# Moving the second group's later statistics chain, and the token weights, in a convolution and scan kernel on one core

## The chip, the cores and the metric

The kernel runs on one core of a Trainium2 chip. The metric is device time in microseconds (us) from the start to the end of one execution. TensorE (PE), VectorE (DVE), ScalarE (ACT), GpSimd (POOL) and the SyncE queue (SP) each run their own list of instructions in order, and wait for one another by semaphores.

## The reference

Input x is 16 images of 256 channels by 1024 pixels, all float32. Two residual blocks follow one another, each behind a group norm (32 groups of 8 channels):

```python
x = x + L0(gn(x))          # mean over pixels -> softmax gate over 8 experts -> sigmoid scale per channel
x = x + L1(gn(x))
# L1, for each image:
xz = silu(in_proj_w @ x + in_proj_b)              # 256 -> 3 * 256: x_ssm, res, gate
xf = silu(depthwise_conv3(x_ssm) + dw_b)
dbc = dbc_w @ xf + dbc_b                          # dt, B, C for 2 heads, 8 states each
xf, dt, B, C = the same in a scan order of the pixels, per head, got by sorting a Moebius map
h[n] = exp(dt[n] * A) * h[n-1] + dt[n] * B[n] * xf[n];  y[n] = C[n] . h[n] + D * xf[n]
y = y back in pixel order
out = silu(out_proj_w @ (y * silu(gate) + res) + out_proj_b)
```

L0 only multiplies each channel of an image by a number. So both group norms and L0 come down to a few parameters for each image and channel, which need the mean and the mean square of every channel of the image first.

## The kernel before, in words

The images are worked on in eight phases of two (`NB = 2`, `PH = 8`), one *cycle* each. In the setup each image is loaded once for its statistics alone. VectorE takes them with `bn_stats` (four passes of 512 elements for two tiles of channels), and for the first `BY_ACT = 5` phases the second tile is taken by ScalarE instead, with two passes of 1024 elements (`statistics(i, b)`, L533 and L534). SP's queue loads the images; phases 6 and 7 go into buffers that phases 3 and 4 used and wait for `stats_done` and `stats_done_a`.

From the statistics come the parameters, in two groups: group 0 is the first four images, group 1 the other twelve. For each group there is a chain of tiny steps across three engines: `combine` (VectorE), `group_sums` (TensorE, a matmul that averages over the channels of a norm group), `normed`, `routes`, `routed`, `experts` and so on for L0; and then the *later chain* for the second norm: `rescaled` (VectorE), `group_sums(g, V_STATS2)` (TensorE), `group_variance` (VectorE), `deviation` (ScalarE, a square root with a table load of its own), `scaled` (VectorE), `shifts` (TensorE, 12 small products), `biases` (VectorE), and `take_params(2)`, which hands phase 2 its parameters, on which GpSimd's `scale_x(2)` waits. For group 1 the matmuls write the PSUM bank `pj[3]`.

The scan over 1024 pixels is done in chunks of 16. For each cycle i and head h:

- `segments(i, h)` on TensorE and `decays(i, h)` on ScalarE make the exponentials (8 activations of 400 elements into `big`). `decays` waits until the scans of the last head are done (`hs_ready`), whose decay factors it overwrites.
- `factors(i, h)` on VectorE makes `bblk`, `turned_factors` makes `cblk`.
- `chunk_sums(i, h, b)` on TensorE (L1411, 8 matmuls with `bblk`) writes the bank `st`, and `scans(i, h, b)` on VectorE runs 8 scans from it into `hs`. There is one bank `st`, so the next `chunk_sums` waits for the last scans.
- `token_products`, `token_weights` and `weights_block` on VectorE build `mblk`, the weights of pixels inside a chunk.
- `results(i, h)` on TensorE: `within` (L1432, with `mblk`), `turn` (L1422, L1423) which transposes `cblk` and `hs` and whose copies ScalarE makes in `turned` (L653), and `from_states` (L1442), which waits for those copies. ScalarE copies the result to `rs` (`result`), and SP stores it.

The order on each engine is written out by hand in its `cycle(i)`. TensorE also has the projections (`project`, `gate`, `residual`, all L1366), `rows` (L1386 and L1388, whose results ScalarE copies in `rows_out`) and `output` (L1491). GpSimd scatters those rows to scan order (`scatter`) and gathers the results back.

## Time and profile before

| what | value |
|---|---|
| median of 3 runs | 877.38 us (875.68 to 877.74) |
| the profiled execution | 875.38 us, of which the profile's span is 872.9 us |
| TensorE busy | 794.8 us (91%) |
| VectorE busy | 571.8 us (66%) |
| ScalarE busy | 557.0 us (64%) |
| GpSimd busy | 372.9 us (43%) |
| mean granted clock of TensorE | 0.96 of full |

The span begins with the first instruction and ends with the last; the execution's own time includes what lies around it. Busy times overlap between engines, so they do not add up to the span. A high busy share is an average over setup, cycles and end, and says nothing of which wait ends last in one of them.

### The profile page before, as it was taken

What the parts mean: (1) busy time and instruction counts of PE and PEld (TensorE: products, weight loads), DVE (VectorE), ACT (ScalarE), POOL (GpSimd) and SP (SyncE); (2) the same over time, 40 slices, a digit from 0 to 9 for tenths busy, and PEclk for the clock granted to TensorE, in tenths of its full rate; (3) what the DMA queues carried; (4) which work ended last, traced back from release to release, by engine and by line L of the source; (5) the groups of instructions that cost most, each with busy time, mean ns of one, the idle gap of its engine ahead of it and who ended that gap; (6) DMA issues with size and microseconds to landing.
All of it is one profiled execution on the core that took longest, in us unless ns stands there. A gap on an engine that the chain in (4) does not pass through costs nothing.

```text
span 872.9 us, 11238 instructions
## 1 busy us (share of the span) xinstructions
PE 794.8 (91%) x3854; PEld 513.4 (59%) x3854; DVE 571.8 (66%) x1048; ACT 557.0 (64%) x1056; POOL 372.9 (43%) x325
## 2 busy tenths in 40 slices
PE   2689867999999999999999999999999999988996
PEld 1356557745675566645684576645684576654852
DVE  5798398467783769276774769275964759178724
ACT  6776645587647856587647846677648846654552
POOL 2394306760288107840388108840487008610240
PEclk9689858999999999999999999999999999999999
DMA  8824671567738293658638393749539463775242
GB/s 330 334 97 149 170 100 62 156 199 84 232 133 238 51 184 141 187 168 98 219 132 241 59 220 114 192 140 134 191 124 256 59 139 125 203 150 134 71 123 97
DMA packets 110986, 136.06 MB, mean 156 GB/s; under 512 B 41801, under 2 KB 91602, under 8 KB 110930
## 3 DMA queue, kind: packets, MB, share of 16 engines
q1 hardware_dynamic: 97040, 99.11, 44.8%
q0 software_dynamic: 12288, 35.80, 12.3%
q8 instruction: 31, 0.51, 0.3%
q10 hardware_dynamic: 1602, 0.45, 0.3%
q14 instruction: 25, 0.20, 0.1%
HBM read 82.76 MB, written 53.61 MB: 156 GB/s over the span
## 4 chain that ended last, share of the span: by engine, by line
PE 68%; ACT 11%; DVE 10%; issue 4%; POOL 4%; DMA 1%; SPq 0%; DVEq 0%; POOLq 0%
PE pj L1366 30%; PE pj L1491 9%; PE pj L1432 6%; PE st L1411 5%; PE tp L1386 5%; ACT big L630 4%; PE tp L1388 4%; PE pj L1442 3%; POOL xt_scratch L434 2%; ACT xf L610 2%; PE tp L1481 2%; DVE big L1121 2%; POOL crow L448 2%; PE tp L1422 2%; ACT L630 1%
## 5 line engine op out<-in xcount | busy, mean ns | idle before, releaser
L1366 PE MATMUL pj<-xb,inw 128*128 128x512 f32 x768 | 340.9, 598 | 0.0
L434 POOL DMA_INDIRECT xt_scratch<-stage,idx x128 | 175.6, 1372 | 344.3 <-issue 333.3
L1366 PEld LDWEIGHTS pj<-xb,inw 128*128 128x128 f32 x768 | 143.7, 191 | 167.0 <-issue 159.6
L448 POOL DMA_INDIRECT crow<-yt_scratch,idx x128 | 135.4, 1058 | 98.9 <-DMA yt_scratch<-rs 59.1
L1017 DVE SCALAR_TENSOR_TENSOR xf<-xs,small,xf 128x1024 f32<-128x1024 f32 x64 | 84.0, 1322 | 108.3 <-ACT xf L603 107.1
L1491 PE MATMUL pj<-gt,outw 128*128 128x512 f32 x256 | 118.2, 593 | 0.6 <-DVE gt L1171 0.6
L653 ACT COPY ch<-tp 128x256 f32<-128x256 f32 x128 | 42.7, 381 | 74.7 <-PE tp L1423 74.6
L1432 PE MATMUL pj<-xp,mblk 128*128 128x128 f32 x512 | 71.7, 285 | 17.0 <-ACT gt L685 8.8
L1177 DVE SCALAR_TENSOR_TENSOR xb<-xb,pcur,rs 128x1024 f32<-128x1024 f32 x32 | 41.0, 1284 | 60.3 <-ACT rs L716 60.3
L642 ACT COPY stage<-tp 128x256 f32<-128x256 f32 x128 | 47.8, 374 | 48.7 <-PE tp L1388 46.4
L1432 PEld LDWEIGHTS pj<-xp,mblk 128*128 128x128 f32 x512 | 64.7, 198 | 23.1 <-ACT gt L685 13.8
L716 ACT ACTIVATE rs<-pj,small 128x512 f32<-128x512 f32 x64 | 44.1, 695 | 49.9 <-PE pj L1491 49.8
L1386 PE MATMUL tp<-dw,xf 128*128 128x162 f32 x256 | 64.9, 338 | 12.1 <-ACT stage L643 11.2
L1386 PEld LDWEIGHTS tp<-dw,xf 128*128 128x128 f32 x256 | 47.5, 210 | 42.1 <-issue 30.9
L630 ACT ACTIVATE big<-sg,small 128x400 f32<-128x400 f32 x128 | 63.7, 609 | 10.5 <-PE sg L1397 10.3
L1491 PEld LDWEIGHTS pj<-gt,outw 128*128 128x128 f32 x256 | 45.9, 190 | 38.1 <-issue 37.0
L1411 PEld LDWEIGHTS st<-bblk,xp 128*128 128x128 f32 x512 | 61.8, 196 | 10.6 <-DVE hs L1077 7.0
L1411 PE MATMUL st<-bblk,xp 128*128 128x64 f32 x512 | 63.1, 278 | 4.0 <-DVE bblk L1103 2.8
L685 ACT ACTIVATE gt<-pj,pcur 128x512 f32<-128x512 f32 x64 | 41.8, 687 | 32.0 <-PE pj L1366 31.8
L1388 PE MATMUL tp<-dw,xf 128*128 128x162 f32 x256 | 61.0, 323 | 0.0
L1121 DVE TENSOR_TENSOR big<-big,crow 128x1024 f32<-128x1024 f32 x32 | 59.8, 1913 | 0.0
L1164 DVE TENSOR_TENSOR gt<-tp,gt 128x512 f32<-128x512 f32 x64 | 41.2, 684 | 24.5 <-PE tp L1481 23.7
(241 smaller groups left out, 1151.6 us busy)
## 6 DMA issues: line engine op xcount, KB each, us to landing
xb<-in_x SPq DMA_DIRECT2D x16, 1024.0 KB, 7.1
xp<-xt_scratch SPq DMA_DIRECT2D x8, 2048.0 KB, 12.6
crow<-cd_scratch SPq DMA_DIRECT2D x128, 128.0 KB, 8.3
yt_scratch<-rs SPq DMA_DIRECT2D x16, 1024.0 KB, 4.9
out<-xb SPq DMA_DIRECT2D x16, 1024.0 KB, 5.6
gt<-in_x SPq DMA_DIRECT2D x4, 1024.0 KB, 11.7
big<-in_x SPq DMA_DIRECT2D x4, 1024.0 KB, 12.1
xp<-xt_scratch SPq DMA_DIRECT2D x8, 272.0 KB, 8.7
```

Of the source, the lines that this page charges most:

```text
L434: pool.indirect_dma_start(out=xt_d.ap(), out_offset=bass.IndirectOffsetOnAxis(ap=idx[:, k:k + 1], axis=0), in_=v(stage, (nt * H + h) * ROW ...
L448: pool.indirect_dma_start(out=v(crow, k * NB * P, (1, NB * P)), out_offset=None, in_=yt_d.ap()[0:(h + 1) * N], in_offset=bass.IndirectOffs ...
L630: last = nc.scalar.activation(v(big, s * EEW, (1, EEW)), v(sg, 0, (1, EEW)), ACT.Exp, scale=v(small, ANEG + h * S + s, (1, 1)))
L642: nc.scalar.copy(v(stage, o + b * P, (ROW, H), (1, P)), v(tp[nt % 2], 0, (P + HK, H), (1, P)))
L1017: nc.vector.scalar_tensor_tensor(dst, tap(k), wt(k), dst, ALU.mult, ALU.add).then_inc(conv_step[ot], 1)
L1121: nc.vector.tensor_tensor(v(big, W_OFF + b * NT * L, (Q * L, S), (L, NT), (1, L)), v(big, SEG + b * NT * L, (EEW, S), (L, NT), (1, L)), v( ...
L1366: last = nc.tensor.matmul(o[:, :], v(inw, ct * 3 * C + col + ot * P, (1, P)), x_view(par, b, ct, nt * HALF, HALF), start=(ct == 0), stop=( ...
L1386: nc.tensor.matmul(v(o, 0, (1, P + HK)), tile(0), v(dw, HK, (1, P + HK)), start=True, stop=False, skip_group_check=True)
L1388: nc.tensor.matmul(v(o, P, (1, HK + P)), tile(1), v(dw, 0, (1, HK + P)), start=False, stop=True, skip_group_check=True).then_inc(x_full, 1)
L1411: last = nc.tensor.matmul(v(st, g * CPT * S, (1, CPT * S)), x_rows(h, b, g), v(bblk, (b * NT + g) * CPT * S, (1, CPT * S)), start=True, st ...
L1432: nc.tensor.matmul(v(pj[2 * b + e], gp * P, (1, P)), v(mblk, (b * NT + g) * P, (1, P)), x_rows(h, b, g), start=(gp == 0), stop=False, skip ...
L1491: last = nc.tensor.matmul(o[:, :], v(outw, h * C + ot * P, (1, P)), v(gt, (b * CT + h) * N + nt * HALF, (1, HALF)), start=(h == 0), stop=( ...
```

## The change

It has three parts, and some moves of buffers that they need.

1. The later chain of group 1 moves back. VectorE ran `rescaled(1)` and `group_variance(1)` ahead of cycle 0 and `scaled(1)` and `biases(1)` around the first head; now `rescaled(1)` and `group_variance(1)` stand behind `factors(0, 1)`, `scaled(1)` behind the scans of head 1, `biases(1)` and `take_params(2)` behind its `weights_block`. On TensorE `group_sums(1, V_STATS2)` moves from behind the first `chunk_sums` to behind `results(0, 0)`, and `shifts(1)` from ahead of `results(0, 0)` to behind the last `chunk_sums`. ScalarE's `deviation(1, V_VAR2)` moves from ahead of cycle 0 to behind the second `result` of head 0. The matmuls now write the bank `sg`, and so wait for `ee_ready`.
2. In cycle 0 and in cycle 7 VectorE makes `token_products` ahead of the first scans and the whole `mblk` ahead of the second scans of head 0.
3. `BY_ACT` is 4: ScalarE's statistics of phase 4 go to VectorE, as four more `bn_stats`, and ScalarE's statistics of image (3, 1) move behind its first `project` steps. On VectorE `statistics(4)` is split in two and moves behind `ranks`, between the bias additions.

The statistics' columns of `rs` move up behind column 2048 and the averaging matrix from `m16` to `rs` (a change of addresses; `result` now waits for `params_ready` at head 1 instead of head 0). The core of the diff:

```diff
@@ build
-        BY_ACT = 5
+        BY_ACT = 4
@@ SP: loads of phases 6 and 7
                 sp.wait_ge(stats_done, i - 2)
-                sp.wait_ge(stats_done_a, (i - 2) * NB)
+                sp.wait_ge(stats_done_a, min(i - 2, BY_ACT) * NB)
                 load_for_statistics(i)
@@ ScalarE, setup
-            for b in range(NB):
-                statistics(3, b)
+            statistics(3, 0)
...
             for ot in range(CT):
                 project(0, 0, 0, ot)
                 first_tap(0, 0, ot)
-            statistics(4, 0)
+            statistics(3, 1)
             convolved(0, 0)
             for ot in range(CT):
                 project(0, 0, 1, ot)
                 first_tap(0, 1, ot)
-            statistics(4, 1)
             rows_out(0, 0)
...
             convolved(1, 1)
-            deviation(1, V_VAR2)
@@ ScalarE, cycle
                 result(i, 0, 0)
                 turned(i, 0, range(4 + AHEAD, 8))
                 result(i, 0, 1)
+                if first(i):
+                    deviation(1, V_VAR2)
                 gate(i, par, range(4, 6))
@@ VectorE, cycle
-                scans(i, 0, 0)
-                if first(i):
-                    scaled(1)
+                if first(i) or last_phase(i):
+
+                    token_products(i, 0)
+                    scans(i, 0, 0)
+                    token_weights(i, 0)
+                    weights_block(i, 0)
+                    scans(i, 0, 1)
                 else:
+                    scans(i, 0, 0)
                     token_products(i, 0)
-                scans(i, 0, 1)
+                    scans(i, 0, 1)
                 if more:
                     add_bias(i + 1, 0, 0, NT)
                     add_bias(i + 1, 1, 0, BIAS_TILES)
                     add_bias(i + 1, 1, BIAS_TILES, BIAS_TILES)
-                token_weights(i, 0)
-                weights_block(i, 0)
+                if not first(i) and not last_phase(i):
+                    token_weights(i, 0)
+                    weights_block(i, 0)
+                factors(i, 1)
                 if first(i):
-                    biases(1, 0, 3 * CT, P_BIAS2, params_ready)
-                    take_params(i + 2)
-                factors(i, 1)
+                    rescaled(1)
+                    group_variance(1, P_SUMS2, V_VAR2)
                 token_products(i, 1)
                 token_weights(i, 1)
                 turned_factors(i, 1)
                 scans(i, 1, 0)
+                if first(i):
+                    scaled(1)
                 weights_block(i, 1)
+                if first(i):
+                    biases(1, 0, 3 * CT, P_BIAS2, params_ready)
+                    take_params(i + 2)
                 scans(i, 1, 1)
@@ VectorE, setup
             convolve(0, 1)
-            statistics(4)
             ties(1)
             ranks()
             add_bias(0, 0, 0, NT)
+            statistics(4, (0,))
+            add_bias(0, 1, 0, BIAS_TILES)
+            statistics(4, (1,))
+            add_bias(0, 1, BIAS_TILES, BIAS_TILES)
             statistics(5)
-            for lo in range(0, NT, BIAS_TILES):
-                add_bias(0, 1, lo, BIAS_TILES)
             statistics(6)
...
             begin(0)
-            rescaled(1)
-            token_products(0, 0)
-            group_variance(1, P_SUMS2, V_VAR2)
@@ TensorE, cycle
                 chunk_sums(i, 0, 0)
-                if not i:
-                    group_sums(1, V_STATS2)
                 segments(i, 1)
...
                 if i:
                     gate(i, par, range(0, 4), last)
-                else:
-                    shifts(1, range(0, CT))
-                    shifts(1, range(CT, 3 * CT))
                 last = four(g_drained, i * G_U + 4)
                 if not i:
 
-                    last[3] = (params_ready, 1)
+                    last[3] = (chain_a, A_CHAIN + A_SIGMOID)
                 results(i, 0, before_t, last, AHEAD, lambda: chunk_sums(i, 1, 0))
                 last = four(r_drained, i * R_U + 4)
+                if not i:
+
+                    pe.wait_ge(ee_ready, H)
+                    group_sums(1, V_STATS2)
                 gate(i, par, range(4, 6), last)
                 last[:2] = four(g_drained, i * G_U + 8)[:2]
                 chunk_sums(i, 1, 1)
+                if not i:
+                    shifts(1, range(0, CT))
+                    shifts(1, range(CT, 3 * CT))
                 results(i, 1, (t_drained, i * T_U + 8), last, 0, lambda: None)
```

Three places of the instruction order follow. In the changed kernel the lines of VectorE count one more, and those of TensorE ten more (L1077 is L1078 there, L1411 is L1421).

VectorE, cycle 0, head 1, from the end of `factors(0, 1)` (`bblk`) to `scans(0, 1, 0)` (`hs`), before:

```order
L1096 TENSOR_TENSOR bc<-xp,big 128x64 x2
L1103 TENSOR_TENSOR bblk<-bc,cst 128x1024
L1121 TENSOR_TENSOR big<-big,crow 128x8x128 x2
L1133 TENSOR_TENSOR big<-big,bc 128x2048
L1138 TENSOR_TENSOR big<-big 128x1024
L1138 TENSOR_TENSOR big<-big 128x512
L1142 SCALAR_TENSOR_TENSOR m<-cst,small,big 128x256
L1146 TENSOR_TENSOR m<-m,big 128x256
L1112 TENSOR_TENSOR cblk<-bc,cst 128x1024
L1077 SCALAR_TENSOR_TENSOR hs<-big,st 128x64 x8
```

The same engine and place in the changed kernel, from the last two steps of `rescaled(1)`:

```order
L966 TENSOR_TENSOR rs<-rs 128x2x12
L967 TENSOR_TENSOR rs<-rs 128x2x12
L916 COPY rs<-sg 128x2x12
L917 TENSOR_TENSOR rs<-rs 128x2x12
L918 TENSOR_TENSOR rs<-sg,rs 128x2x12
L919 TENSOR_SCALAR rs<-rs 128x2x12
L1122 TENSOR_TENSOR big<-big,crow 128x8x128 x2
L1134 TENSOR_TENSOR big<-big,bc 128x2048
L1139 TENSOR_TENSOR big<-big 128x1024
L1139 TENSOR_TENSOR big<-big 128x512
L1143 SCALAR_TENSOR_TENSOR m<-cst,small,big 128x256
L1147 TENSOR_TENSOR m<-m,big 128x256
```

Between `bblk` and `token_products` (`big<-big,crow`) now stand the eleven steps of `rescaled(1)`, of which two are shown, and the four of `group_variance(1)`, the first of which (`rs<-sg`) reads what TensorE's `group_sums` writes.

TensorE, cycle 0, from the last `from_states` of head 0 (`pj<-ch`) through two gates (`pj<-xb,inw`) to `results(0, 1)`, before:

```order
L1442 MATMUL pj<-ch 128x128 x8
L1366 MATMUL pj<-xb,inw 128x512 x4
L1411 MATMUL st<-bblk,xp 128x64 x8
L1422 MATMUL tp<-dw,cblk 128x128
L1423 MATMUL tp<-dw,hs 128x128
```

The same place in the changed kernel:

```order
L1452 MATMUL pj<-ch 128x128 x8
L1299 MATMUL sg<-rs 128x48
L1376 MATMUL pj<-xb,inw 128x512 x4
L1421 MATMUL st<-bblk,xp 128x64 x8
L1331 MATMUL sg<-rs,inw 128x12 x12
L1432 MATMUL tp<-dw,cblk 128x128
L1433 MATMUL tp<-dw,hs 128x128
```

`group_sums` (`sg<-rs`, one matmul) now stands ahead of the gates, and the twelve of `shifts` (`sg<-rs,inw`) between the last `chunk_sums` (`st<-bblk,xp`) and `results(0, 1)`.

VectorE, the start of cycle 7, behind `output(6, b)`, before:

```order
L1077 SCALAR_TENSOR_TENSOR hs<-big,st 128x64 x8
L1121 TENSOR_TENSOR big<-big,crow 128x8x128 x2
L1077 SCALAR_TENSOR_TENSOR hs<-big,st 128x64 x8
L1133 TENSOR_TENSOR big<-big,bc 128x2048
L1138 TENSOR_TENSOR big<-big 128x1024
L1138 TENSOR_TENSOR big<-big 128x512
L1142 SCALAR_TENSOR_TENSOR m<-cst,small,big 128x256
L1146 TENSOR_TENSOR m<-m,big 128x256
L1154 TENSOR_TENSOR mblk<-m,cst 128x2048
```

In the changed kernel:

```order
L1122 TENSOR_TENSOR big<-big,crow 128x8x128 x2
L1078 SCALAR_TENSOR_TENSOR hs<-big,st 128x64 x8
L1134 TENSOR_TENSOR big<-big,bc 128x2048
L1139 TENSOR_TENSOR big<-big 128x1024
L1139 TENSOR_TENSOR big<-big 128x512
L1143 SCALAR_TENSOR_TENSOR m<-cst,small,big 128x256
L1147 TENSOR_TENSOR m<-m,big 128x256
L1155 TENSOR_TENSOR mblk<-m,cst 128x2048
L1078 SCALAR_TENSOR_TENSOR hs<-big,st 128x64 x8
```

The first scans (`hs<-big,st`) stand behind `token_products`, and the second ones behind all that makes `mblk`.

## Rows read from the trace of the kernel before

**Rows 1.** The page, part 4: shares by engine of the chain that ended last.
```profile
PE 68%; ACT 11%; DVE 10%; issue 4%; POOL 4%; DMA 1%; SPq 0%; DVEq 0%; POOLq 0%
```

**Rows 2.** Timeline of TensorE, setup: start us, us, instruction, idle before.
```profile
59.67 0.91 PE L1386 MATMUL tp<-dw,xf 128*128 128x162 f32 x2 [3.85 <-ACT stage L643]
...
96.98 0.42 PE L1289 MATMUL pj<-rs,m 128*128 128x48 f32 x2 [0.78 <-ACT gt L685]
```

**Rows 3.** Timeline of ScalarE, setup.
```profile
57.10 1.04 ACT L533 ACTIVATE hs<-big 128x1024 f32<-128x1024 f32 x1
...
93.22 1.98 ACT L685 ACTIVATE gt<-pj,pcur 128x512 f32<-128x512 f32 x3
```

**Rows 4.** Timeline of VectorE, setup.
```profile
62.56 2.46 DVE L879 BATCH_NORM_STATS2 rs<-big 128x6 f32<-128x512 f32 x4
...
76.14 0.30 DVE L1023 TENSOR_TENSOR stage<-stage,small 128x136 f32<-128x136 f32 x1 [2.40 <-ACT stage L643]
...
81.11 2.59 DVE L1017 SCALAR_TENSOR_TENSOR xf<-xs,small,xf 128x1024 f32<-128x1024 f32 x2
```

**Rows 5.** Timeline of SP's queue, setup.
```profile
65.04 0.88 SPq L309 DMA_DIRECT2D big<-in_x  x2
```

**Rows 6.** The page, part 6: DMA issues, KB each, us to landing.
```profile
big<-in_x SPq DMA_DIRECT2D x4, 1024.0 KB, 12.1
```

**Rows 7.** Timeline of TensorE, cycle 0.
```profile
136.22 2.74 PE L1321 MATMUL pj<-rs,inw 128*128 128x12 f32 x24
143.88 2.05 PE L1432 MATMUL pj<-xp,mblk 128*128 128x128 f32 x8 [4.92 <-DVE mblk L1154]
...
149.55 1.90 PE L1411 MATMUL st<-bblk,xp 128*128 128x64 f32 x16
...
154.75 3.70 PE L1366 MATMUL pj<-xb,inw 128*128 128x512 f32 x8
158.28 1.89 PE L1411 MATMUL st<-bblk,xp 128*128 128x64 f32 x16
```

**Rows 8.** Timeline of VectorE, cycle 0.
```profile
122.01 0.17 DVE L956 TENSOR_SCALAR rs<-rs 128x24 f32<-128x24 f32 x1
...
124.13 3.70 DVE L1121 TENSOR_TENSOR big<-big,crow 128x1024 f32<-128x1024 f32 x2
...
136.14 2.31 DVE L1133 TENSOR_TENSOR big<-big,bc 128x2048 f32<-128x2048 f32 x1
...
145.16 1.22 DVE L1103 TENSOR_TENSOR bblk<-bc,cst 128x1024 f32<-128x1024 f32 x1
...
156.45 1.52 DVE L1077 TENSOR_TENSOR_SCAN hs<-big,st 128x64 f32<-128x64 f32 x8
```

**Rows 9.** Timeline of ScalarE, cycle 0.
```profile
136.81 1.28 ACT L630 ACT_TABLE_LOAD   x1
138.11 3.98 ACT L630 ACTIVATE big<-sg,small 128x400 f32<-128x400 f32 x8
```

**Rows 10.** Windows: stretch, length, busy us by engine, TensorE's granted clock, DMA.
```profile
121.00:124.50 3.50, 3.39 (x16) 3.42 (x17) 3.22 (x13) 2.68 (x3) 0.00 (x0) 0.50 0.43 56
...
143.80:148.00 4.20, 4.12 (x22) 4.03 (x22) 4.06 (x9) 0.74 (x2) 3.29 (x4) 0.57 0.26 96
```

**Rows 11.** Timeline of TensorE, cycle 7.
```profile
793.69 2.00 PE L1411 MATMUL st<-bblk,xp 128*128 128x64 f32 x16 [0.88 <-DVE hs L1077]
...
806.32 2.05 PE L1432 MATMUL pj<-xp,mblk 128*128 128x128 f32 x8 [3.32 <-DVE mblk L1154]
...
820.60 1.89 PE L1411 MATMUL st<-bblk,xp 128*128 128x64 f32 x16
```

**Rows 12.** Timeline of VectorE, cycle 7.
```profile
793.55 3.71 DVE L1121 TENSOR_TENSOR big<-big,crow 128x1024 f32<-128x1024 f32 x2
...
818.49 1.52 DVE L1077 TENSOR_TENSOR_SCAN hs<-big,st 128x64 f32<-128x64 f32 x8
```

**Rows 13.** Timeline of ScalarE, cycle 7.
```profile
801.60 3.98 ACT L630 ACTIVATE big<-sg,small 128x400 f32<-128x400 f32 x8
```

More of the change, by code:

```diff
@@ L141, in build @@
         W1G, B1G, W2, B2 = 0, 272, 408, 664
-        BN, A_SUM, A_SQ, MEAN, SQ, T, SQR = 928, 1312, 1328, 1344, 1376, 1408, 1440
-        VAR, MG, TMP, SC, RSTD, A_, B_, HID = 1568, 1600, 1632, 1664, 1696, 1728, 1760, 1792
-        GROUP_AT = 128
+        BN, A_SUM, A_SQ, MEAN, SQ, T, SQR = 2048, 2432, 2448, 2464, 2496, 2528, 2560
+        VAR, MG, TMP, SC, RSTD, A_, B_, HID = 2688, 2720, 2752, 2784, 2816, 2848, 2880, 2912
+        GROUP_AT = 3200
         STAGED = (xb[0], xb[1], xb[2], gt, big, xp, gt, big)
-        BY_ACT = 5
+        BY_ACT = 4
         TIES, LATER, BASE, RANK = 16, 32, 48, 64
@@ L512, in _ @@
             act.dma_start(v(rseg, 0, (1, P)), const_d[:, CONST_W:CONST_W + P]).then_inc(weights_in, 16)
-            act.dma_start(v(m16, GROUP_AT, (1, P)), const_d[:, CONST_W + P:CONST_W + 2 * P]).then_inc(weights_in, 16)
+            act.dma_start(v(rs, GROUP_AT, (1, P)), const_d[:, CONST_W + P:CONST_W + 2 * P]).then_inc(weights_in, 16)
             act.dma_start(v(rs, W1G, (136, CT), (1, 136)), w1g_d).then_inc(weights_in, 16)
@@ L527, in statistics @@
                 image = i * NB + b
-                spare = (v(xf[b], 0, (1, N)), v(xf[b], N, (1, N))) if i < 4 else (v(hs, 0, (1, N)), v(ch, 0, (1, N)))
-                wait(act, stats_done_a, image - 1 if i < 4 else image)
+                spare = v(xf[b], 0, (1, N)), v(xf[b], N, (1, N))
+                wait(act, stats_done_a, image - 1)
                 act.wait_ge(x_landed(i, b), 16)
@@ L658, in result @@
                     wait(act, out_ready, i * NB * CT)
-                    if first(i):
-                        act.wait_ge(params_ready, 1)
+                if first(i) and h == 1 and b == 0:
+                    act.wait_ge(params_ready, 1)
                 act.wait_ge(ch_used, i * T_U + (h * NB + b) * 4 + 4)
@@ L872, in ties, with statistics @@
                 link(last)
-            def statistics(i):
-                for b in range(NB):
+            def statistics(i, images=range(NB)):
+                for b in images:
                     dve.wait_ge(x_landed(i, b), 16)
@@ L879, in statistics @@
                             last = nc.vector.bn_stats(v(rs, BN + (ct * B + i * NB + b) * 12 + half * 6, (1, 6)), staged(i, b, ct, half * HALF, HALF))
-                last.then_inc(stats_done, 1)
+                if images[-1] == NB - 1:
+                    last.then_inc(stats_done, 1)
             def cols(g, at, tiles=CT):
@@ L884, in cols, with bank @@
                 return v(rs, at + lo, (B, tiles), (1, n))
-            def bank(g):
-                return pj[3] if g else st
+            def bank(g, later=False):
+                return (sg if later else pj[3]) if g else st
             def combine(g):
@@ L912, in group_variance @@
                 n = GROUPS[g][1]
-                mean, square = (v(bank(g), k * CT * n, (n, CT), (1, n)) for k in range(2))
+                mean, square = (v(bank(g, given == P_SUMS2), k * CT * n, (n, CT), (1, n)) for k in range(2))
                 dve.wait_ge(chain_p, g * P_CHAIN + given)
@@ L982, in biases @@
                 dve.wait_ge(chain_p, g * P_CHAIN + given)
-                nc.vector.tensor_tensor(home(g, PRM_BIAS + lo, (1, count)), v(bank(g), 128 + lo * n, (n, count), (1, n)),
+                nc.vector.tensor_tensor(home(g, PRM_BIAS + lo, (1, count)), v(bank(g, True), 128 + lo * n, (n, count), (1, n)),
                                         v(small, INB + lo, (1, count), (0, n)), ALU.add).then_inc(semaphore, 1)
@@ L1187, in cycle @@
                     take_params(i + 2)
-                scans(i, 0, 0)
-                if first(i):
-                    scaled(1)
+                if first(i) or last_phase(i):
[4 more added lines that the diff above has]
+                    scans(i, 0, 1)
                 else:
+                    scans(i, 0, 0)
                     token_products(i, 0)
-                scans(i, 0, 1)
+                    scans(i, 0, 1)
                 if more:
@@ L1281, in _, with bank @@
         def _(pe):
-            def bank(g):
-                return pj[3] if g else st
+            def bank(g, later=False):
+                return (sg if later else pj[3]) if g else st
             def group_sums(g, taken):
@@ L1288, in group_sums @@
                 pe.wait_ge(chain_v, g * V_CHAIN + taken)
-                nc.tensor.matmul(v(bank(g), 0, (1, 2 * CT * n)), v(m16, GROUP_AT, (1, P)), v(rs, MEAN + lo, (B, 2 * CT), (1, n)),
+                nc.tensor.matmul(v(bank(g, taken == V_STATS2), 0, (1, 2 * CT * n)), v(rs, GROUP_AT, (1, P)), v(rs, MEAN + lo, (B, 2 * CT), (1, n)),
                                  start=True, stop=True).then_inc(chain_p, 1)
@@ L1320, in shifts @@
                     for ct in range(CT):
-                        last = nc.tensor.matmul(v(bank(g), 128 + ot * n, (1, n)), v(inw, ct * 3 * C + ot * P, (1, P)),
+                        last = nc.tensor.matmul(v(bank(g, True), 128 + ot * n, (1, n)), v(inw, ct * 3 * C + ot * P, (1, P)),
                                                 v(rs, T + ct * B + lo, (1, n)), start=(ct == 0), stop=(ct == CT - 1))
```

## The prediction, made before the changed kernel ran

> **What bounds the kernel now.** I read the chain that ended last first: 68% of it is TensorE and only 11% and 10% are ScalarE and VectorE [rows 1]. So a microsecond counts only where TensorE waits, or where its clock is low. Next I read TensorE's timeline for idle time in brackets. In the setup it waits 3.85 us at 59.67 for the ScalarE copies, and it starts `group_sums(1)` at 96.98 behind ScalarE's gates [rows 2]. In cycle 0 it waits 4.92 us for `mblk` and starts at 143.88 [rows 7]. In cycle 7 it waits 3.32 us for `mblk` and starts at 806.32 [rows 11]. These are the three places the change aims at. Last I read VectorE and ScalarE in those stretches. All times below called "now" are positions in the old trace; "new" ones are worked out.
>
> The clock view gives the price of a stop. TensorE ran at half (1.2 GHz) in 121.0 to 124.5, and at 0.57 of full for the 4.2 us behind the 4.92 us wait [rows 10]. Half speed over 4 us of work costs about 2 us, so a new stop of several us costs up to 2 us beside its length.
>
> **Setup.** ScalarE drops one pair of statistics passes ahead of `rows_out(0, 0)`: 57.10 to the copies that released TensorE at 59.67, about 2.1 us [rows 3, 2]. (The other pair is only replaced by `statistics(3, 1)`, of the same two instructions.) TensorE's `rows`, `count` and projections therefore start 2.1 us earlier. VectorE pays: `statistics(4)` grows from 4 to 8 passes, and 4 took 2.46 us [rows 4]. Its wait of 2.40 us at 76.14 [rows 4] does not swallow this, because both `statistics(4)` pieces now stand ahead of the bias additions, between waits for ScalarE copies that themselves come 2.1 us earlier. I count `convolve(1, 0)` at 83.9 instead of 81.11. ScalarE's second projections reuse `xs` and wait for it, and its four gates, now from 93.22, slide behind the second `convolve(1, 0)` tile and `convolved(1, 0)`: they end near 96.3 instead of 96.9. VectorE itself, with `statistics(7)` from 89.1 and `combine(1)`, is done near 95.7. So of 2.1 us some **0.6 us** reach `group_sums(1)` (0 if VectorE slips a little more, 2.1 if nothing does). The load of phase 7 moves on SP's queue from 65.04 [rows 5] to about 74.0, since it waits for `statistics(4)`; its median of 12.1 us to landing [rows 6] ends at 86, ahead of 89.1. The later load falls on the scatter; I price that at nothing while it lands by 89.
>
> **Cycle 0, first half.** New times, 0.6 us early. VectorE is free at 121.4 (now 122.01), does `token_products` in 3.7, `scans(0,0,0)` in 1.5, and then what ran from 136.14 to 143.7, 7.6 us [rows 8, 7]. `mblk` is ready at 134.2 and `scans(0,0,1)` at 135.7. TensorE loses `group_sums` and reaches `within` at about 135.2 (the 2.74 us of `shifts` that stood at 136.22 are gone from here). So the 4.92 us wait vanishes and `within` starts 8.7 us early. It doesn't last: `from_states` needs the copies `turned(2)` and `turned(3)`, which stand on ScalarE behind `decays(0, 1)`. That is a table load at 136.81 and 3.98 us from 138.11 [rows 9]; TensorE's 1.2 us make it 135.6, and the exponentials end at 140.9. TensorE therefore stops for some 3 us and ends `from_states(b0)` near 142.2.
>
> One rule speaks about that load. The Trainium skill, "ScalarE: Activation LUTs", section "What ACT_TABLE_LOAD costs", gives 1.28 us and 1.38 us of drain for each switch. The load here took 1.28 us and the next activation began 0.02 us after it [rows 9]. By the page each of the two loads that stand ahead of `decays` (cycles 0 and 7) would hold up the chain 1.4 us more and the time would be near 895; I go by the row.
>
> **Cycle 0, second half.** Three things follow each other.
> (a) `factors(0, 1)` waits for `decays`, so `bblk` is ready at 142.8 (now 146.4, [rows 8]). Then VectorE runs `rescaled(1)`, 2.1 us as from 122.01 to 124.13 [rows 8], done at 144.9, and its next instruction is `group_variance(1)`, which waits for `group_sums` on TensorE. TensorE has that matmul behind all of `results(0, 0)`: from `chunk_sums` to the end took 149.55 to 154.75, 5.2 us, at full clock [rows 7]. From 142.8 that is 148.0, and with the low clock behind the 3 us stop up to 150; I take 149.3. VectorE stands 4 to 5 us, and behind it stand `token_products(0,1)`, `token_weights`, `turned_factors` and the scans that TensorE needs.
> (b) `group_variance` sees the sum at 149.8 and takes 0.85 (four operations at 0.2, as the eleven of 122.01). From `bblk` to the end of `scans(0,1,0)` took 146.38 to 157.97, 11.6 us [rows 8]. New end: 150.7 + 11.6 = 162.3. TensorE's gates (3.70 us [rows 7]) are over near 153.3, so it stops 9 us, then starts `chunk_sums(0,1,1)` at 162.3 instead of 158.28 [rows 7]: **+4.0 us**.
> (c) The stop drops the clock: `chunk_sums` takes about 1.7 us more (1.89 at full clock), and `shifts`, 2.74 us [rows 7], now stands alone on the path ahead of `results(0, 1)`, partly at half clock, 0.9 more: **+5.3 us**.
> Together +9.3 us at the end of cycle 0, with the 0.6 in it. By bounds: at full clock throughout, +2.6 and +2.7, or 5.3; with every pass of (a) to (c) at half clock, +5.0, +1.9 and +5.5, or 12.4. Moving `deviation` with its two table loads to between `result(0,0,1)` and the gates has 9 us of TensorE's stop as cover; without the cover it would cost 1.5. `take_params(2)` comes near 169.9 and POOL's `scale_x(2)` ends by 175, ahead of TensorE's project near 181, so POOL and the y gathers stay hidden. From cycle 1 on TensorE is the chain, so nothing gives the 9.3 back.
>
> **Cycle 7.** VectorE came free at 792.1: `token_products` began at 793.55 behind 1.5 us of scans [rows 12]. New: products to 795.8, `scans(7,0,0)` to 797.3, weights and `mblk` to 804.8, `scans(7,0,1)` to 806.2. The order costs twice. First, `chunk_sums(7,0,1)` waits until 797.3 instead of 793.69 [rows 11]; TensorE stops 4.5 us and loses 2 us of clock, so it reaches `within` at 808.5, where `mblk` waits already: about +2 against 806.32, of which the former slow start there pays back most. Second, `decays(7, 1)` waits for `scans(7,0,1)` and for ScalarE's two gates, which TensorE now makes later: it starts at 807.0 instead of 801.60 [rows 13] and ends at 811.0. `bblk` 1.9 later, then the same 11.6 us: `scans(7,1,0)` end at 824.5; they ended at 820.0 [rows 12]. TensorE, done with its gates at 821.8, starts `chunk_sums(7,1,1)` at 824.5 instead of 820.60 [rows 11], **+3.9 us**, and loses **1.6 us** of clock after the 2.7 us stop. Bounds 3.4 (bound by the scans alone) and 7. Together **+5.5 us**.
>
> **Sum.** 9.3 + 5.5 = 14.8 us. The profiled execution took 875.4 us around its span of 872.9; with 14.8 it would take 890.2. The median of the runs is 2.0 us above it, so I predict **892.2 us**. What measurement tells from no change is about 0.3%, 2.6 us.
>
> **Rivals.**
> A, the clock holds: TensorE's stops of 3, 9 and 4 us leave its clock up. Against it stand the half-speed stretches behind each long wait; for it, waits of under 1 us cost nothing. The sum is then 5.3 + 3.9, or 886.6. Chance 0.13.
> B, cycle 7 is covered: `decays(7, 1)` is not late, because ScalarE and TensorE catch up in the gates. Only 9.3 stays: 886.7. Against it: its wait on the scans of image 1 is in the code. Chance 0.1.
> C, faster: the h=1 chain of VectorE is not what TensorE waits for, because `group_sums` is reached when `rescaled` is done. It decides at a point: if the sum is on TensorE by 145 and `scans(0,1,0)` by 153, TensorE keeps the 5.4 us it gains at the end of `results(0, 0)` (149.3 against 154.75), pays 2.7 for `shifts`, and keeps 1.5 more of setup. With cycle 7 at zero that is 877.4 - 4.0 = 873.4. Against it: VectorE has 11.6 us of work there that nothing shortens. Chance 0.06.
> D, the change comes out even: the setup keeps 2.1, the clock holds, and cycle 7 is covered; 5.3 - 1.5 leaves 3.8, and a `bblk` 2 us earlier makes it 879. Chance 0.06.
> E, setup loses: the phase 7 load or VectorE's longer queue makes `statistics(7)` the last at `group_sums(1)`, 2 to 4 us later than now; 895 to 897. For it: that queue has no idle time left. Chance 0.12.
> My forecast has the remaining 0.53.
>
> **The numbers.** The likeliest case reaches from 888 to 896; A, B and E take it to 883 and 898. Below lie C and D, above all bounds at once. Faster 0.06, same 0.05, slower 0.89.
>
> **What would show it.** After the change: TensorE's waits name `hs` scans ahead of `chunk_sums(0,1,1)` (about 9 us) and `chunk_sums(7,0,1)` (4.5 us), no long wait on `mblk`; VectorE waits some 4.5 us for TensorE's `sg` matmul ahead of `group_variance`; `group_sums(1)` in the setup starts 0.6 us earlier; cycles 1 to 6 are as they were, shifted. I am wrong if `scans(0,1,0)` end before 158, or if the clock stays at full after these stops.

## The result, and the profile after

The changed kernel took 895.34 us (median of 4 runs, 894.66 to 896.89) against 876.53 us for the kernel before (4 runs, 875.29 to 877.74): 1.0217 times as long, with a 95% interval of 1.0195 to 1.0239. The profiled execution has a span of 892.7 us, 19.8 more than before.

The page of the changed kernel, parts 1 and 4 (the second line answers to [rows 1]):

```profile
PE 804.5 (90%) x3854; PEld 520.1 (58%) x3854; DVE 574.4 (64%) x1052; ACT 553.3 (62%) x1048; POOL 369.7 (41%) x325
...
PE 62%; DVE 14%; ACT 13%; issue 5%; POOL 4%; DMA 1%; SPq 0%; DVEq 0%; POOLq 0%; ACTq 0%
```

TensorE has as many instructions as before but is busy 9.7 us longer: that is clock, not work. The rest of the 19.8 us, some 10, is new idle time, and the chain that ended last passes from TensorE (68% before) to VectorE and ScalarE.

To see where, four marks are enough: the first `chunk_sums` of a cycle and the first gate behind its last `results`. Timeline of TensorE, kernel before:

```profile
121.11 3.65 PE L1411 MATMUL st<-bblk,xp 128*128 128x64 f32 x16 [2.78 <-DVE bblk L1103]
...
167.77 4.56 PE L1366 MATMUL pj<-xb,inw 128*128 128x512 f32 x10
...
789.99 1.90 PE L1411 MATMUL st<-bblk,xp 128*128 128x64 f32 x16
...
830.08 8.42 PE L1366 MATMUL pj<-xb,inw 128*128 128x512 f32 x19
```

Timeline of TensorE, changed kernel, cycle 0 (answers to [rows 7]):

```profile
116.40 3.65 PE L1421 MATMUL st<-bblk,xp 128*128 128x64 f32 x16 [2.78 <-DVE bblk L1104]
...
137.07 1.07 PE L1452 MATMUL pj<-ch 64*128 64x128 f32 x8 [3.67 <-ACT ch L652]
138.98 3.51 PE L1421 MATMUL st<-bblk,xp 128*128 128x64 f32 x16
148.23 0.42 PE L1299 MATMUL sg<-rs 128*128 128x48 f32 x2
...
161.33 3.68 PE L1421 MATMUL st<-bblk,xp 128*128 128x64 f32 x16 [9.17 <-DVE hs L1078]
164.80 5.24 PE L1331 MATMUL sg<-rs,inw 128*128 128x12 f32 x24
180.05 2.41 PE L1376 MATMUL pj<-xb,inw 128*128 128x512 f32 x5
```

and cycle 7 (answers to [rows 11]):

```profile
802.86 1.90 PE L1421 MATMUL st<-bblk,xp 128*128 128x64 f32 x16
810.15 3.67 PE L1421 MATMUL st<-bblk,xp 128*128 128x64 f32 x16 [4.47 <-DVE hs L1078]
...
838.73 2.13 PE L1421 MATMUL st<-bblk,xp 128*128 128x64 f32 x16 [2.58 <-DVE hs L1078]
...
849.96 1.55 PE L1376 MATMUL pj<-xb,inw 128*128 128x512 f32 x3
```

By subtraction:

| stretch | before | after | difference |
|---|---|---|---|
| start to first `chunk_sums` of cycle 0 | 121.1 | 116.4 | -4.7 |
| cycle 0, to the gate behind `results(0, 1)` | 46.7 | 63.7 | +17.0 |
| from there to the first `chunk_sums` of cycle 7 | 622.2 | 622.8 | +0.6 |
| cycle 7, to the gate behind `results(7, 1)` | 40.1 | 47.1 | +7.0 |

Both waits for `mblk` are gone, and in cycle 0 three others came for the one removed (two of TensorE, 3.67 and 9.17 us, and one of VectorE, 8.07 us). VectorE and ScalarE, cycle 0, timeline (answers to [rows 8, 9]):

```profile
136.79 0.41 DVE L1093 TENSOR_TENSOR bc<-bc,big 128x128 f32<-128x128 f32 x1 [4.39 <-ACT big L629]
...
140.51 0.18 DVE L967 TENSOR_TENSOR rs<-rs 128x24 f32<-128x24 f32 x1
...
148.76 0.18 DVE L916 COPY rs<-sg 128x24 f32<-128x24 f32 x1 [8.07 <-PE sg L1299]
...
149.62 3.71 DVE L1122 TENSOR_TENSOR big<-big,crow 128x1024 f32<-128x1024 f32 x2
...
159.75 1.52 DVE L1078 TENSOR_TENSOR_SCAN hs<-big,st 128x64 f32<-128x64 f32 x8
```
```profile
131.47 1.28 ACT L629 ACT_TABLE_LOAD   x1 [0.53 <-DVE hs L1078]
132.77 3.99 ACT L629 ACTIVATE big<-sg,small 128x400 f32<-128x400 f32 x8
```

Read as a chain: TensorE reaches `from_states` and waits 3.67 us for copies that stand on ScalarE behind `decays(0, 1)`; VectorE ends `rescaled(1)` at 140.7 and waits 8.07 us for one matmul that TensorE has queued behind `results(0, 0)`; then TensorE waits 9.17 us for the scans that stand on VectorE behind that. Windows of the changed kernel (columns as in [rows 10]) show the clock:

```profile
142.20:148.50 6.30, 6.30 (x41) 5.95 (x40) 0.00 (x0) 0.89 (x3) 4.80 (x5) 0.58 0.33 120
...
161.30:165.00 3.70, 3.67 (x18) 3.67 (x18) 3.01 (x6) 0.00 (x0) 0.00 (x0) 0.50 0.00 0
165.00:170.00 5.00, 5.00 (x26) 5.00 (x26) 0.00 (x0) 0.00 (x0) 0.00 (x0) 0.50 0.00 0
170.00:174.00 4.00, 4.00 (x21) 4.00 (x21) 1.90 (x10) 1.49 (x4) 3.10 (x3) 0.50 0.00 0
174.00:180.00 6.00, 6.00 (x62) 5.56 (x61) 0.00 (x0) 2.18 (x6) 4.92 (x6) 0.93 0.16 46
```

Behind the 9.17 us stop TensorE stands at 1.2 GHz (0.50 of 2.4) for 12.7 us in which it never waits.

### The profile page after: what moved, and what is told of

Its sections match the earlier page's. It is cut to its first block, busy times and chain, and to the rows that moved or that the text cites. A ratio compares the mean times of both kernels' runs of the same rounds, so it can differ in the third digit from the quotient of the medians.

```text
span 892.7 us, 11232 instructions
## 1 busy us (share of the span) xinstructions
PE 804.5 (90%) x3854; PEld 520.1 (58%) x3854; DVE 574.4 (64%) x1052; ACT 553.3 (62%) x1048; POOL 369.7 (41%) x325
## 4 chain that ended last, share of the span: by engine, by line
PE 62%; DVE 14%; ACT 13%; issue 5%; POOL 4%; DMA 1%; SPq 0%; DVEq 0%; POOLq 0%; ACTq 0%
PE pj L1376 25%; PE pj L1501 9%; PE pj L1442 6%; PE st L1421 6%; ACT big L629 5%; PE tp L1396 3%; PE pj L1452 3%; PE tp L1398 3%; POOL xt_scratch L434 3%; DVE xf L1018 2%; DVE rs L878 2%; DVE big L1122 2%; ACT L629 2%; PE tp L1432 2%; ACT xf L609 2%
## 5 line engine op out<-in xcount | busy, mean ns | idle before, releaser
L434 POOL DMA_INDIRECT xt_scratch<-stage,idx x128 | 171.8, 1342 | 348.1 <-issue 299.8
L1018 DVE SCALAR_TENSOR_TENSOR xf<-xs,small,xf 128x1024 f32<-128x1024 f32 x64 | 83.9, 1322 | 109.6 <-ACT xf L602 108.4
L1501 PE MATMUL pj<-gt,outw 128*128 128x512 f32 x256 | 118.3, 593 | 0.6 <-DVE gt L1172 0.6
L1421 PE MATMUL st<-bblk,xp 128*128 128x64 f32 x512 | 68.5, 292 | 19.4 <-DVE hs L1078 16.2
L1421 PEld LDWEIGHTS st<-bblk,xp 128*128 128x128 f32 x512 | 66.6, 209 | 26.9 <-DVE hs L1078 23.0
L641 ACT COPY stage<-tp 128x256 f32<-128x256 f32 x128 | 47.9, 375 | 50.2 <-PE tp L1398 47.2
L1442 PEld LDWEIGHTS pj<-xp,mblk 128*128 128x128 f32 x512 | 66.5, 203 | 14.5 <-ACT gt L684 13.8
L1396 PE MATMUL tp<-dw,xf 128*128 128x162 f32 x256 | 62.0, 325 | 10.0 <-ACT stage L642 9.1
L1396 PEld LDWEIGHTS tp<-dw,xf 128*128 128x128 f32 x256 | 44.6, 199 | 40.6 <-issue 30.9
L1398 PE MATMUL tp<-dw,xf 128*128 128x162 f32 x256 | 58.1, 310 | 0.0
```

What stands on the lines that cost most here:

```text
L434: pool.indirect_dma_start(out=xt_d.ap(), out_offset=bass.IndirectOffsetOnAxis(ap=idx[:, k:k + 1], axis=0), in_=v(stage, (nt * H + h) * ROW ...
L641: nc.scalar.copy(v(stage, o + b * P, (ROW, H), (1, P)), v(tp[nt % 2], 0, (P + HK, H), (1, P)))
L1018: nc.vector.scalar_tensor_tensor(dst, tap(k), wt(k), dst, ALU.mult, ALU.add).then_inc(conv_step[ot], 1)
L1396: nc.tensor.matmul(v(o, 0, (1, P + HK)), tile(0), v(dw, HK, (1, P + HK)), start=True, stop=False, skip_group_check=True)
L1398: nc.tensor.matmul(v(o, P, (1, HK + P)), tile(1), v(dw, 0, (1, HK + P)), start=False, stop=True, skip_group_check=True).then_inc(x_full, 1)
L1421: last = nc.tensor.matmul(v(st, g * CPT * S, (1, CPT * S)), x_rows(h, b, g), v(bblk, (b * NT + g) * CPT * S, (1, CPT * S)), start=True, st ...
```

## The experiments

Each was timed against the kernel before on the same chip. "Off" is the ratio less one, times the median of before there (873.95 to 876.53 us). It is not quite the difference of the two medians: for e10 they lie 8.1 us apart where off is 6.6. Kernels are compared by off, since before itself differed between these sets of runs. Cycle 0 and cycle 7 are measured between the marks above, in the one profiled execution. That one can lie at an end of its runs: those of e6 and e7 are the slowest of theirs (895.72 and 879.73 us), that of e8 is nearly the fastest (873.67).

| kernel | median us (runs) | ratio [95%] | off us | cycle 0 | cycle 7 |
|---|---|---|---|---|---|
| before | 876.53 (4) | | | 46.7 | 40.1 |
| the change | 895.34 (4) | 1.0217 [1.0195, 1.0239] | +19.0 | 63.7 | 47.1 |
| e1_setup_only | 872.51 (12) | 0.9977 [0.9960, 0.9993] | -2.0 | 47.4 | 40.2 |
| e2_old_last | 888.77 (4) | 1.0161 [1.0127, 1.0194] | +14.1 | 62.5 | 40.1 |
| e3_variance_behind | 882.11 (4) | 1.0100 [1.0061, 1.0140] | +8.7 | 51.7 | 46.6 |
| e4_busy | 891.94 (4) | 1.0187 [1.0150, 1.0225] | +16.4 | 60.6 | 46.5 |
| e5_busy_to_end | 889.61 (4) | 1.0162 [1.0128, 1.0197] | +14.2 | 56.4 | 46.9 |
| e6_chain_only | 894.08 (4) | 1.0205 [1.0167, 1.0243] | +18.0 | 65.4 | 42.1 |
| e7_weights_first_0 | 875.98 (12) | 1.0006 [0.9986, 1.0026] | +0.5 | 48.0 | 42.1 |
| e8_behind_old_last | 877.04 (10) | 1.0016 [0.9997, 1.0036] | +1.4 | 51.6 | 40.1 |
| e9_setup_weights_0 | 872.83 (12) | 0.9985 [0.9970, 1.0001] | -1.3 | 47.9 | 40.2 |
| e10_last_only | 882.03 (6) | 1.0075 [1.0047, 1.0103] | +6.6 | 46.7 | 46.6 |
| e11_sums_early | 887.16 (4) | 1.0142 [1.0111, 1.0173] | +12.4 | 56.2 | 46.9 |

**e1_setup_only** is the kernel before with part 3:

```diff
-        BY_ACT = 5
+        BY_ACT = 4
@@ ScalarE, setup
-            for b in range(NB):
-                statistics(3, b)
+            statistics(3, 0)
...
-            statistics(4, 0)
+            statistics(3, 1)
```

> The kernel before with part 3 of the change alone (BY_ACT 4, statistics (3, 1) behind the first project steps, statistics(4) split behind ranks). Theory: in the changed kernel this part gave 4.7 us, since cycle 0 began at 116.4 instead of 121.1, and nothing behind it gives that back while TensorE is the chain, so 4 to 5 us faster than before, about 872. Rival, my prediction as it stood: 0.6 us at most, about 876; the rest of the 4.7 would have come from the chain's move.

It is 2.0 us faster: more than nothing, less than the 4.7 of the changed kernel's profile and than the 4 to 5 that I expected. Timeline of TensorE in the changed kernel, setup (answers to [rows 2]):

```profile
57.58 0.54 PE L1396 MATMUL tp<-dw,xf 128*128 128x162 f32 x2 [1.71 <-ACT stage L642]
...
71.01 20.96 PE L1376 MATMUL pj<-xb,inw 128*128 128x512 f32 x48
...
93.50 0.42 PE L1299 MATMUL pj<-rs 128*128 128x48 f32 x2 [1.53 <-ACT gt L684]
```

The `rows` start 2.09 us earlier, and each takes 0.54 instead of 0.91 us: the stop ahead of them is 1.71 instead of 3.85 us, and most of them take 0.44 us, as ahead of that stop, where most took 0.75 in the kernel before. `group_sums(1)` starts 3.48 us earlier (93.50 instead of 96.98). The same setup began cycle 0 between 116.40 and 120.04 in the nine traces that hold part 3 (mean 118.3), and the old one between 121.11 and 123.15 in four (mean 122.1). So the profile shown drew the early end. The rest between 3.8 and 2.0 us may lie in the interval (0.6 to 3.5) and in cycle 0, which is 0.7 longer in this trace. ScalarE's wait for `xf` that I expected is there:

```profile
84.10 1.27 ACT L595 ACTIVATE xs<-pj,pcur 128x512 f32<-128x512 f32 x2 [4.15 <-DVE xf L1018]
```

**e2_old_last** is the changed kernel with the old order of VectorE in cycle 7.

```diff
-                if first(i) or last_phase(i):
+                if first(i):
...
-                if not first(i) and not last_phase(i):
+                if not first(i):
```

> The changed kernel with the old order in cycle 7 (weights first only in cycle 0). Theory: cycle 7 took 47.1 us from its first chunk_sums to the end of results instead of 40.1, so 7 us faster than the changed kernel, about 888.5. Rival: the delay is only shifted (ScalarE or the gates make it up either way), so under 2 us.

The off time falls by 4.9 us, from 19.0 to 14.1 (each with an interval of 2 to 3 us each way), and cycle 7 in the trace by the whole 7.0. The medians alone, 6.6 us apart, say more than they should: before was 1.8 us faster in these runs. TensorE's timeline is that of [rows 11] again, with the 3.3 us wait for `mblk` that the change had removed:

```profile
820.11 1.18 PE L1442 MATMUL pj<-xp,mblk 128*128 128x128 f32 x8 [3.33 <-DVE mblk L1155]
```

**e10_last_only** makes the test from the other side: the kernel before, with the new order in cycle 7 alone.

```diff
+                if last_phase(i):
+                    token_products(i, 0)
                 scans(i, 0, 0)
-                if first(i):
+                if last_phase(i):
+                    token_weights(i, 0)
+                    weights_block(i, 0)
+                elif first(i):
                     scaled(1)
...
-                token_weights(i, 0)
-                weights_block(i, 0)
+                if not last_phase(i):
+                    token_weights(i, 0)
+                    weights_block(i, 0)
```

> The kernel before, with the new order of VectorE in cycle 7 alone (token_products ahead of the first scans, mblk ahead of the second ones). Taking this order out of the changed kernel gave back some 7 us. If cycle 7's loss stands by itself, this kernel is 6 to 7 us slower than before (near 882), with chunk_sums(7,0,1) waiting 4.5 us and the scans of head 1 ending late. The rival: the loss needs the state in which the changed cycle 0 leaves the queues; then it is under 3 us slower.

It is 6.6 us slower (4.1 to 9.0), cycle 7 takes 6.5 us longer in the trace, and TensorE shows the two waits of the changed kernel to 0.01 us:

```profile
798.13 3.68 PE L1417 MATMUL st<-bblk,xp 128*128 128x64 f32 x16 [4.46 <-DVE hs L1077]
...
826.21 2.59 PE L1417 MATMUL st<-bblk,xp 128*128 128x64 f32 x16 [2.58 <-DVE hs L1077]
```

Cycle 7's loss stands by itself.

**e3_variance_behind** is the changed kernel with `group_variance(1)` behind `scans(0, 1, 0)`, so that the scans no longer stand behind TensorE's `group_sums`.

```diff
                     rescaled(1)
-                    group_variance(1, P_SUMS2, V_VAR2)
...
                 scans(i, 1, 0)
                 if first(i):
+                    group_variance(1, P_SUMS2, V_VAR2)
                     scaled(1)
```

> The changed kernel with group_variance(1) moved on VectorE from behind rescaled(1) to behind scans(0, 1, 0), so that token_products and the rest don't stand behind TensorE's group_sums. Theory: VectorE's wait of 8.07 us goes, scans(0, 1, 0) end near 152.4 instead of 161.3, TensorE's stop of 9.17 us goes, and with it its half clock, so results(0, 1) end 12 to 15 us earlier: about 881. Rival: the chain only waits elsewhere (ScalarE's gates behind deviation, or mblk), and under 5 us come back.

The place of this one step, four small operations, is worth 10.3 us of the 19.0 by the off times. Timeline of TensorE:

```profile
153.94 2.00 PE L1421 MATMUL st<-bblk,xp 128*128 128x64 f32 x16 [0.87 <-DVE hs L1078]
155.77 3.44 PE L1331 MATMUL sg<-rs,inw 128*128 128x12 f32 x24
```

The wait of 9.17 us is 0.87, and cycle 0 takes 51.7 us instead of 63.7. It is not back at 46.7: `chunk_sums(0, 1, 1)` to the gate still took 15.5 us, 3.3 more than in e5 below, where nothing waits.

**e11_sums_early** cures the same wait from TensorE's side: VectorE's order is that of the change, and the matmul stands inside `results(0, 0)`.

```diff
-                results(i, 0, before_t, last, AHEAD, lambda: chunk_sums(i, 1, 0))
+                results(i, 0, before_t, last, AHEAD, lambda: (chunk_sums(i, 1, 0), early_sums(i)))
                 last = four(r_drained, i * R_U + 4)
-                if not i:
-                    pe.wait_ge(ee_ready, H)
-                    group_sums(1, V_STATS2)
```

> The changed kernel, with group_sums(1) on TensorE directly behind chunk_sums(0,1,0), inside results(0,0), instead of behind it. Theory: VectorE's 8.07 us wait ahead of group_variance came from the place of this matmul in TensorE's queue behind half-clocked results; chunk_sums(0,1,0) ended at 142.5 in the changed kernel's trace, so the wait falls to about 2 us, the scans of head 1 end 5.9 us earlier, TensorE's stop ahead of chunk_sums(0,1,1) falls from 9.2 to about 3 us, and with some 1.5 us of clock the median is near 888 (886 to 890). Rival: TensorE is held at this place for rescaled(1) or for the bank sg, and the wait only changes engines; then it stays above 893.

Timeline of TensorE and of VectorE:

```profile
143.45 0.61 PE L1299 MATMUL sg<-rs 128*128 128x48 f32 x2
...
156.75 3.12 PE L1421 MATMUL st<-bblk,xp 128*128 128x64 f32 x16 [4.14 <-DVE hs L1078]
159.67 5.24 PE L1331 MATMUL sg<-rs,inw 128*128 128x12 f32 x24
```
```profile
144.16 0.18 DVE L916 COPY rs<-sg 128x24 f32<-128x24 f32 x1 [2.15 <-PE sg L1299]
```

VectorE's wait fell from 8.07 to 2.15, TensorE's stop from 9.17 to 4.14, and the off time by 6.6 us: the queue place was the cause, as the theory said. But `shifts` still took 5.24 us, behind a stop of 4.14 as behind one of 9.17.

**e4_busy** and **e5_busy_to_end** price the clock. Both are the changed kernel with 9 and 11 matmuls of 512 columns, of which nothing is read, ahead of `chunk_sums(0, 1, 1)`, in the time in which TensorE stopped.

```diff
                 last[:2] = four(g_drained, i * G_U + 8)[:2]
+                if not i:
+                    pe.wait_ge(r_drained, 4)
+                    for _ in range(9):
+                        nc.tensor.matmul(pj[2][:, :], v(inw, 0, (1, P)), x_view(0, 0, 0, 0, HALF), start=True, stop=True)
                 chunk_sums(i, 1, 1)
```

> The changed kernel with nine more matmuls of 512 columns on TensorE ahead of chunk_sums(0, 1, 1), whose results nothing reads, in place of most of the 9.17 us stop; the output is unchanged. Theory: the clock is up when the scans are done, so chunk_sums (3.68 us), shifts (5.24) and the first half of results(0, 1) run at full clock and 5 to 7 us come back: about 889. Rival, that the low clock costs nothing beside the wait: no change, 895, or slower by what sticks out of the stop.

> As e4_busy with eleven matmuls instead of nine, so that TensorE has nearly no stop ahead of chunk_sums(0, 1, 1). In e4_busy a stop of 1.48 us was left and shifts still ran at half clock (5.24 us). Theory: with no stop the clock stays up through shifts and the start of results(0, 1): 3 to 5 us faster than e4_busy, about 888. Rival: the clock falls in shifts whatever stands ahead of it, since its matmuls are 12 columns wide; then as e4_busy, 892.

Timeline of TensorE with 9 matmuls, then with 11:

```profile
152.98 7.89 PE L1545 MATMUL pj<-xb,inw 128*128 128x512 f32 x18
162.34 2.29 PE L1421 MATMUL st<-bblk,xp 128*128 128x64 f32 x16 [1.48 <-DVE hs L1078]
164.43 5.24 PE L1331 MATMUL sg<-rs,inw 128*128 128x12 f32 x24
```
```profile
154.83 9.61 PE L1545 MATMUL pj<-xb,inw 128*128 128x512 f32 x22
164.27 1.92 PE L1421 MATMUL st<-bblk,xp 128*128 128x64 f32 x16
166.03 2.80 PE L1331 MATMUL sg<-rs,inw 128*128 128x12 f32 x24
```

With 9, a stop of 1.48 us is left; `chunk_sums` still runs near full clock, and `shifts` behind it at half. Less came back than I expected: 2.6 us by the off times, within the noise, and 3.0 in cycle 0. With 11 no stop is left, `shifts` takes 2.80 us, and cycle 0 takes 56.4 instead of 63.7 us although TensorE does 9.6 us of useless work in it. From the start of `chunk_sums(0, 1, 1)` to the gate it is 12.2 us instead of 18.7, so 6.5 of these 7.2 us are the low clock behind that one stop; the other 0.7 lie ahead of it. By the off times 4.8 us came back, with intervals of 2 to 3 us each way.

**e6_chain_only** is the kernel before with part 1 alone; the diff is part 1 of the one shown above.

> Part 1 of the change alone: the later chain of group 1 in its new place, with the old statistics and the old order of weights and scans in cycles 0 and 7. Theory: VectorE's wait for group_sums and the shifts on the path are this part's alone, so nearly all of the loss of cycle 0 is here, 12 to 16 us slower than before, about 889. Rival: the loss needs the new order of scans and weights (decays held back by scans(0, 0, 1)); then under 8 us.

It lost 18.0 us (14.6 to 21.3), more than the 12 to 16 that I had expected. TensorE, cycle 0:

```profile
144.56 2.04 PE L1438 MATMUL pj<-xp,mblk 128*128 128x128 f32 x8 [7.48 <-DVE mblk L1157]
...
168.76 3.67 PE L1417 MATMUL st<-bblk,xp 128*128 128x64 f32 x16 [9.18 <-DVE hs L1080]
```

`shifts` used to fill part of the time before `mblk` [rows 7]; with it gone TensorE waits 7.48 us there instead of 4.92, and the second stop is that of the full change. What part 1 costs in cycle 0 is 18.7 us here, in the slowest of its four runs. The parts taken alone add up to -2.0 + 18.0 + 0.5 + 6.6 = 23.1 us (e1, e6, e7, e10) against 19.0 for the change; with intervals of 2 to 3 us on most of them, it is not shown whether part 2 makes part 1 cheaper.

**e7_weights_first_0** is the kernel before with part 2's order in cycle 0 alone.

```diff
+                if first(i):
+                    token_weights(i, 0)
+                    weights_block(i, 0)
                 scans(i, 0, 1)
...
-                token_weights(i, 0)
-                weights_block(i, 0)
+                if not first(i):
+                    token_weights(i, 0)
+                    weights_block(i, 0)
```

> The kernel before with the weights ahead of the second scans in cycle 0 alone, the chain and the rest as before. Theory: mblk comes some 5 us earlier and the 4.92 us wait goes, but from_states then waits for the copies behind decays(0, 1), and decays now waits for scans(0, 0, 1) near 139; so 0 to 2 us gained, about 875. Rival, what the order is for: the whole wait of 4.9 us and its clock come back, 5 to 6 us, about 870. Other side: decays so late that head 1 loses what head 0 wins, 2 us slower.

No difference. Timeline of TensorE and of ScalarE:

```profile
147.77 1.23 PE L1446 MATMUL pj<-ch 64*128 64x128 f32 x8 [3.78 <-ACT ch L653]
149.83 3.52 PE L1415 MATMUL st<-bblk,xp 128*128 128x64 f32 x16
```
```profile
142.17 1.28 ACT L630 ACT_TABLE_LOAD   x1 [3.32 <-DVE hs L1077]
```

The wait of 4.92 us for `mblk` is gone, and one of 3.78 us for the copies has come a few instructions later, because `decays(0, 1)` waits for the scans that were put behind the weights. The stop changed its name, and the half clock behind it stayed.

**e8_behind_old_last** joins e3 and e2.

> e3_variance_behind and e2_old_last together: the changed kernel with group_variance(1) behind scans(0, 1, 0) and the old order in cycle 7. Theory: the two add up, 13 and 7 us off the changed kernel: about 875, level with before within 3 us. Rival: they overlap, over 878.

Within the interval it equals the kernel before: the two waits that the change makes are most of its loss. What is left of part 1, 4.9 us of cycle 0, is `shifts` in front of `results(0, 1)` (2.7 at full clock) and the low clock behind a stop of 1.52 us; the earlier setup pays for most of it.

**e9_setup_weights_0** joins e1 and e7.

> The kernel before, with the statistics of part 3 moved to VectorE and, in cycle 0 alone, the weights of head 0 ahead of its second scans; the later chain stays where it was and cycle 7 too. The first edit alone gave 2 us, the second alone nothing. If they add up, this kernel is 2 us faster than before (near 873). Rival: an earlier start lets the second edit show its worth, and 4 to 5 us come together (near 871).

They add up and nothing more comes of it: 1.3 us, against 2.0 and -0.5. Part 3 alone is the best version found; none of the others beats it.

## Why the prediction was right, and where its terms were off

The median came 3.1 us above my 892.2 and inside the range, by the mechanism forecast: each wait that I named is in the trace under the name I gave it, `scans(0, 1, 0)` ended at 161.27 and not before 158, and cycles 1 to 6 only shifted. One of the signs failed: `group_sums(1)` in the setup started 3.5 us earlier and not 0.6. The loss forecast was 14.8 us, the ratio makes it 19.0 and the two traces 19.8.

That the number fell inside the range was partly luck. The terms were less exact than the sum, because errors of both signs stood in it. By the traces cycle 0 cost 7.1 us more than forecast and cycle 7 1.5 more, with 0.6 between them; the setup gave 4.1 more than forecast. Had it given only my 0.6, the time would have been 901 us by the traces, above the 898 of the range, and about 898 with the 2.0 us that e1 measured.

**Setup**: I took -0.6 of bounds from 0 to 2.1. ScalarE's earlier start was 2.09 us, as worked out. That VectorE would eat most of it was wrong: `convolve(1, 0)` began at 81.43 and not 83.9, and `group_sums` was released by ScalarE's gates. And the lower stop gave the clock back in the `rows`, which the sum did not have. The runs show 2.0 us (0.6 to 3.5). My rival E, that the setup loses, fell.

**Cycle 0, (a)**: `decays`, `bblk` and `rescaled(1)` ended as far behind the first `chunk_sums` as I had put them (140.7 is 24.3 us behind it, I had 24.4). The first mis-sized piece is `group_sums`: 31.8 us behind that mark instead of 28.8. I had let `results(0, 0)` run mostly at full clock behind the 3.67 us stop, and it ran at 0.58. So VectorE stood 8.07 us and not 4 to 5.

**(b)**: the 11.6 us behind it held (149.62 to 161.27), and TensorE stopped 9.17 us where I had 9. But the stop was pushed back by the same 3 us.

**(c)**: from the start of `chunk_sums(0, 1, 1)` to the gate took 18.7 us against 9.5 before, 9.2 more where I had 5.3. I had `shifts` only partly at half clock, and nothing behind it. All of `shifts` (5.24 us) and the first 4 us of `results(0, 1)` were at 0.50. Shown by e5: without the stop `shifts` is 2.80 us, and the stretch to the gate is 6.5 us shorter. So the step that was sized worst is the price of a stop: "up to 2 us beside its length" was 6.5 us here, where the sum had 2.6.

Together these make 17.0 for my 9.9 (9.3 with the setup's 0.6 taken out), and that is above the bound of 12.4 (13.0 from the mark), which was too low as it stood. For (a) it gave `results(0, 0)` only 1 us more than the forecast did, though 5.2 us of work at half clock take 10.4; and for (c) it had no low clock behind `shifts`.

**Cycle 7**: 5.5 forecast, 7.0 in the trace, and by the off times 4.9 (e2) and 6.6 (e10). The stop of 4.5 us was 4.47. `decays(7, 1)` was late as said. The timeline of ScalarE and the wait on VectorE (answers to [rows 13, 12]):

```profile
819.86 1.28 ACT L629 ACT_TABLE_LOAD   x1
821.15 3.99 ACT L629 ACTIVATE big<-sg,small 128x400 f32<-128x400 f32 x8
```
```profile
825.17 0.37 DVE L1093 TENSOR_TENSOR bc<-bc,big 128x128 f32<-128x128 f32 x1 [5.91 <-ACT big L629]
```

The exponentials begin 18.3 us behind the first `chunk_sums`, where it was 11.6 [rows 13 and the mark at 789.99]: 6.7 us later, and I had 5.4. The 1.3 us stand in full in the start of `chunk_sums(7, 1, 1)`, 5.3 us later where I had 3.9; its stop (2.58 us, I had 2.7) and the clock behind it (1.75 us from there to the gate, I had 1.6) were sized rightly. Some 1 us of the 1.3 is the gates ahead of `decays(7, 1)`, 8.08 us instead of 7.03. Rival B, that this is covered, fell.

**The rule on table loads** was weighed against a row, and the rows after agree with the row: the load at 131.47 took 1.28 us and the next activation began 0.02 us after it, and so it was at 819.86. The 1.38 us of drain that the Trainium skill ("ScalarE: Activation LUTs", "What ACT_TABLE_LOAD costs") adds is not between them here, nor ahead of the second load, which began 0.02 us behind the gate; the 895 that it would have given was met for other reasons, the mis-sized terms above.

**Rival A**, that the clock holds, fell by the windows and by e5. What spoke for it, that waits under 1 us cost nothing, held in the kernel before (0.88 us at 793.69 [rows 11]) but not in e3, where the stretch behind a stop of 0.87 us took 3.3 us more than without one. **C** decided at `scans(0, 1, 0)` ending by 153; in e3 they end near it (153.9), and even so that kernel is 8.7 us slower, most of which is cycle 7's: with the old cycle 7 (e8) it is even, not faster. (C's own terms add to 4.2 us, not 4.0.) **D** fell with A and B.

What stays open: why the same setup begins cycle 0 at times 3.6 us apart; no run was made for it. In cycle 7, where e6 and e7 have the old order and took 2 us more, the traces show where but not why: behind the same wait of 0.88 us the gates ahead of `decays(7, 1)` took 8.5 and 8.4 us at a granted clock of 0.82 and 0.83, against 7.0 us at 1.00 before, and `chunk_sums(7, 1, 1)` then waited 1.7 us for scans, where it had waited for nothing.
